# A graph-attention kernel: masks of two chunks made in place over a ring of six adjacency chunks, and a front with six row buffers

## What is computed

```
h    = relu(layernorm(x))
neib = tanh(neigh @ Wn1 + bn1) @ Wn2 + bn2            # 4096 x 32
val  = neigh @ Wv + bv                                # 4096 x 128
att  = tanh(h @ Wx1 + bx1) @ Wx2 + bx2                # 4096 x 32
ws   = leaky_relu(att @ neib.T, 0.01)                 # 4096 x 4096
ws   = softmax(where(adj > 0, ws, -9e15), axis=1)
out  = x + concat([h @ Wfx + bfx, ws @ val], axis=1)
```

## Time and profile before

| | |
|---|---|
| median of three runs | 505.74 us |
| the profiled execution: its own time, its span | 505.33 us, 503.5 us |
| TensorE matmul busy | 474.3 us (94%) |
| ScalarE busy | 434.8 us (86%) |
| VectorE busy | 425.3 us (84%) |
| GpSimd busy | 213.5 us (42%) |
| the masks, L663 | 128 instructions, 63.3 us and 1.7 us busy |

### The profile page before, as it was taken

The page is one execution under the profiler, slowest core; times in us unless marked ns, Lnnn a source line. Parts: engine busy times, 40 slices in busy tenths (PEclk is TensorE's granted clock), DMA queues, the critical chain, the costliest instruction groups (busy, mean ns, idle before and its releaser), DMA issues.

```text
span 503.5 us, 9162 instructions
## 1 busy us (share of the span) xinstructions
PE 474.3 (94%) x2964; PEld 368.3 (73%) x3007; DVE 425.3 (84%) x824; ACT 434.8 (86%) x625; POOL 213.5 (42%) x341
## 2 busy tenths in 40 slices
PE   6888898999999999999999999999999999998996
PEld 4767666776777677777777778777777787766884
DVE  1449898999898999999898989899998989994664
ACT  1675999999999899989999899989999999987552
POOL 1441042445644673457445663476445534540100
PEclk9999999999999999999999999999999999999999
DMA  8995475464567435755566356754564556500100
GB/s 232 269 217 105 102 127 87 78 141 77 85 120 172 77 59 100 159 111 86 78 133 142 67 85 126 168 83 62 97 142 81 85 105 125 85 1 1 43 2 21
DMA packets 38191, 52.04 MB, mean 103 GB/s; under 512 B 4096, under 2 KB 29952, under 8 KB 38144
## 3 DMA queue, kind: packets, MB, share of 16 engines
q0 software_dynamic: 9216, 33.56, 40.0%
q1 hardware_dynamic: 27856, 17.83, 11.8%
q10 hardware_dynamic: 1072, 0.07, 0.1%
HBM read 80.81 MB, written 4.19 MB: 169 GB/s over the span
## 4 chain that ended last, share of the span: by engine, by line
PE 64%; ACT 12%; issue 9%; DVE 8%; DMA 4%; POOL 2%; ACTq 1%; DVEq 0%; SPq 0%
PE ps_turned L924 17%; PE ps_scores L901 10%; PE ps_product L943 8%; PE ps_product L945 8%; PE ps_product L944 8%; PE ps_scores L900 4%; ACT pt_hi L516 3%; ACT scores L555 3%; ACT scores L543 3%; DVE scores L692 3%; PE ps_product L870 2%; DVE pt_lo L674 2%; DMA b<-in_L_gnn_bx 2%; POOL scores L419 2%; DMA x_left<-in_x 1%
## 5 line engine op out<-in xcount | busy, mean ns | idle before, releaser
L674 DVE TENSOR_TENSOR pt_lo<-ps_turned,pt_hi 128x512 fp32r<-128x512 f32 x256 | 172.9, 686 | 39.6 <-ACT pt_hi L516 20.6
L419 POOL TENSOR_TENSOR scores<-scores,mask 128x512 f32<-128x512 f32 x109 | 126.9, 1165 | 171.8 <-ACT scores L543 171.7
L516 ACT ACTIVATE pt_hi<-ps_turned 128x512 fp32r<-128x512 f32 x256 | 156.1, 610 | 37.7 <-PE ps_turned L924 37.2
L924 PE MATMUL ps_turned<-ident,scores 128*128 128x128 f32 x1024 | 154.6, 273 | 2.5 <-DVE pt_lo L674 2.3
L924 PEld LDWEIGHTS ps_turned<-ident,scores 128*128 128x128 f32 x1024 | 123.8, 140 | 44.2 <-DVE pt_lo L674 15.1
L543 ACT ACTIVATE scores<-ps_scores 128x1024 f32<-128x1024 f32 x128 | 132.4, 1035 | 5.7 <-PE ps_scores L901 5.7
L555 ACT ACTIVATE scores<-scores,neg_top 128x2048 f32<-128x2048 f32 x64 | 129.4, 2022 | 0.0
L692 DVE CUSTOM_DVE_ANT_0 scores<-ps_scores,scores,top 128x1024 f32<-128x1024 f32 x96 | 122.5, 1276 | 3.3 <-ACT scores L543 3.0
L943 PE MATMUL ps_product<-pt_hi,v_hi 128*128 128x512 f32 x256 | 122.1, 477 | 0.2 <-DVE pt_lo L674 0.2
L901 PE MATMUL ps_scores<-neib,xs 128*128 128x512 f32 x256 | 108.8, 502 | 3.7 <-DVE top L692 1.3
L945 PE MATMUL ps_product<-pt_lo,v_hi 128*128 128x512 f32 x256 | 101.4, 396 | 0.0
(11 more groups left out here) (76 smaller groups left out, 367.1 us busy)
## 6 DMA issues: line engine op xcount, KB each, us to landing
adj_in<-in_adj POOLq DMA_DIRECT2D x62, 512.0 KB, 5.4
scores<-in_L_gnn_neigh SPq DMA_DIRECT2D x8, 512.0 KB, 6.6
x_rows<-in_x SPq DMA_DIRECT2D x8, 512.0 KB, 3.7
x_left<-in_x SPq DMA_DIRECT2D x8, 256.0 KB, 6.7
x_right<-in_x SPq DMA_DIRECT2D x8, 256.0 KB, 2.9
out_h<-x_left SPq DMA_DIRECT2D x8, 256.0 KB, 3.4
out_h<-x_right SPq DMA_DIRECT2D x8, 256.0 KB, 3.4
scores<-in_adj POOLq DMA_DIRECT2D x2, 512.0 KB, 9.9
```

Source lines behind the costliest of these rows:

```text
L419: pool.tensor_tensor(half, half, mask[:, s % MASK_RING, BANK:CHUNK], ALU.add).then_inc(masked, 1)
L516: act.activation(pt_hi[:, (2 * b + u) % HI_RING], pt[:, u], ACT.Copy).then_inc(hi_done, 1)
L674: dve.tensor_tensor(pt_lo[:, u], pt[:, u], pt_hi[:, (2 * b + u) % HI_RING].bitcast(FP32), ALU.subtract).then_inc(lo_done, 1)
L924: last = pe.transpose(pt[:, u, i * P:(i + 1) * P], scores[:, parity * TILES + i, n * P:(n + 1) * P], ident[:, :])
```

## The change

The ring of masks goes. A mask of two chunks (2048 columns) is made by one VectorE instruction, in place over the two chunks of adjacency that one DMA has loaded, on even steps; TensorE and GpSimd read the masks there. The ring of adjacency has six chunks, and a pair is loaded anew when its scores and GpSimd's additions are done (on odd steps). The front has six row buffers; x_ahead is gone, and the statistics of x group 1 are made from x_rows, by VectorE in the last front step. The diagonal copies of the second-layer weights are made by VectorE from one small DMA each (spread_w2), most small weights move from ScalarE's queue to SyncE's, the wait for biases is split by side, ScalarE runs a Tanh on the identity before its first copy, and TensorE turns the identity some more times as filler (WARM_UP, FILL). The order of some pieces within a step changes on every engine, and the steps of the x work shift.

```diff
-ADJ_RING = 4
+ADJ_RING = 6
-MASK_RING = 3
-ROWS_RING = 5
+ROWS_RING = 6
-TURN_X = 5
-PACE = (4, 5, 6, 7)
+TURN_X = 4
+FILL = (6, 6, 4, 0, 0, 0, 0, 0)
-X_LOAD = -8
-X_STATS = (-6, -6, -6, -4)
+X_LOAD = -9
+X_STATS = (-6, -6, -5, -4)
-X_RSTD = (-3, -2, -1, -1)
-X_NORM = (0, 1, 2, 4)
+X_RSTD = (-4, -3, -2, -1)
+X_NORM = (2, 2, 4, 4)
-X_LEFT_LOAD, X_SUM = 11, (10, 13)
-X_RIGHT = 7
-V_START, V_STRIDE = 1, 2
+X_LEFT_LOAD, X_SUM = 16, (12, 14)
+X_RIGHT = 8
+V_START, V_STRIDE = 0, 2
+LEFT_0 = 4
-WARM_UP = 12
+WARM_UP = 15
...
+            def load_w2(side, w_in):
+                sp.dma_start(w2_raw[:, side, :], w_in.rearrange("(r p) h -> r p h", r=1).to_broadcast(
+                    [TILES, D_HID, D_HID])).then_inc(w2_in[side], 16)
...
# SyncE: n0 n1 x0 w2n n2 b2n n3 w1x n4 b1x w2x b2x n5, then n6, n7 as buffers come free, w_fx, w_v
+            sp.wait_ge(x_turned, KT)
+            load_x_rows(1)
# ... then the wide biases, x_left(0), x_right(0)
...
# GpSimd, front
+            pool.wait_ge(rows_in[(NEIGH_GROUPS - 2) % ROWS_RING], 32)
+            load_adj(0)
+            pool.wait_ge(rows_in[(NEIGH_GROUPS - 1) % ROWS_RING], 32)
+            load_adj(LOAD)
+            pool.wait_ge(x_rows_in, 32)
+            load_adj(2 * LOAD)
+            load_adj(3 * LOAD)
             for i in range(NEWTON + 1):
                 rstd_of(1, i)
+            load_adj(4 * LOAD)
...
# GpSimd, step: right_sum, left_sum, then the addition of the mask, then
+                gone = s - LOAD + 1
+                n = gone + ADJ_RING + (FRONT if gone < ADJ_RING else 0)
+                if gone % LOAD == 0 and 0 <= gone and n < STEPS and not ADJ_RING <= gone < ADJ_RING + FRONT:
+                    pool.wait_ge(scored, s + 1)
+                    if s >= POOL_MASKS:
+                        pool.wait_ge(masked, s + 1 - POOL_MASKS)
+                    load_adj(n)
...
# ScalarE, front: only w1_n and b1_n on its queue
+            act.wait_ge(made, 1)
+            act.activation(agg[:, 0:1], ident[:, 0:1], ACT.Tanh)
             turned_copy(0)
-            act.wait_ge(b1_in, B1_IN)
+            act.wait_ge(b1_in[0], 16)
...
# ScalarE, step: aggregate, hi 0, rise, hi 1, power, side
# VectorE, front step 7
+                if e == NEIGH_GROUPS - 1:
+                    for i in range(TILES):
+                        x_stats(1, i)
+                    x_aggr(1)
...
             def mask_of(n):
+                if n % LOAD or n >= STEPS:
+                    return
...
+                pair = adj_of(n, LOAD).rearrange("p a n -> p (a n)")
+                dve.tensor_scalar(pair, pair, 0.0, MASKED, ALU.is_le, ALU.mult).then_inc(mask_done, 1)
...
# VectorE, step: leak, lo 0, x_work, close, negate, lo 1, neigh_rest, mask_of(s + 2)
# TensorE: warm(FILL[e]) ahead of first_layer; product(s, -1) and agg_turn come ahead of side
-                    pe.wait_ge(mask_done, k + 1)
+                    pe.wait_ge(mask_done, s // LOAD + 1)
```

More of the change, by code:

```diff
@@ L107, in build @@
         adj_in = sb("adj_in", [P, ADJ_RING, CHUNK], BF16)
-        mask = sb("mask", [P, MASK_RING, CHUNK], BF16)
         xs = sb("xs", [P, 2, GROUP], FP32R)
@@ L148, in scratch @@
             return ap.rearrange(f"p ({names}) -> p {names}", **sizes)
-        rows = [scratch(4, i * TILES * D_IN, TILES, D_IN) for i in range(4)] + [scratch(5, 0, TILES, D_IN)]
-        x_ahead = scratch(5, 1024, TILES, D_IN)
+        rows = [scratch(4, i * TILES * D_IN, TILES, D_IN) for i in range(4)] + [scratch(5, i * TILES * D_IN, TILES, D_IN) for i in range(2)]
         hidden = scratch(5, 2048, 2, P)
@@ L242, in chunk_of, with adj_place, adj_of, mask @@
             return s // GSTEPS % 2, s // CHUNKS % TILES, s % CHUNKS
+        def adj_place(n):
+            return n if n < ADJ_RING else n - FRONT
+        def adj_of(n, chunks):
+            if ADJ_RING <= n < ADJ_RING + FRONT:
+                return adj_front[:, n - ADJ_RING:n - ADJ_RING + chunks, :]
+            i = adj_place(n) % ADJ_RING
+            return adj_in[:, i:i + chunks, :]
+        def mask(n):
+            return adj_of(n, 1).rearrange("p a n -> p (a n)")
         def v_halves(v, half):
@@ L413, in step @@
             def step(s):
+                for i in range(2):
+                    if (g := right_due(s - i)) is not None:
+                        right_sum(g, i)
+                for i in range(2):
+                    if e := x_due(s, X_SUM[i]):
+                        left_sum(e, i)
                 if POOL_MASKS <= s < STEPS:
@@ L418, in step @@
                     half = scores[:, parity * TILES + tile, c * CHUNK + BANK:(c + 1) * CHUNK]
-                    pool.tensor_tensor(half, half, mask[:, s % MASK_RING, BANK:CHUNK], ALU.add).then_inc(masked, 1)
-                n = s + ADJ_RING + (FRONT if s < FRONT else 0)
-                if s % LOAD == 0 and n < STEPS and not FRONT <= s < ADJ_RING + FRONT:
-                    pool.wait_ge(mask_done, s + LOAD)
-                    load_adj(n)
-                for i in range(2):
-                    if e := x_due(s, X_SUM[i]):
-                        left_sum(e, i)
-                for i in range(2):
-                    if (g := right_due(s - i)) is not None:
-                        right_sum(g, i)
+                    pool.tensor_tensor(half, half, mask(s)[:, BANK:CHUNK], ALU.add).then_inc(masked, 1)
+                gone = s - LOAD + 1
[4 more added lines that the diff above has]
+                        pool.wait_ge(masked, s + 1 - POOL_MASKS)
+                    load_adj(n)
                 for i in range(NEWTON + 1):
@@ L645, in _ @@
             x_aggr(0)
[L646 to L648 removed]
+            for side in range(2):
+                dve.wait_ge(b2_in[side], 16)
             def mask_of(n):
[L652 removed]
+                if n % LOAD or n >= STEPS:
+                    return
                 if ADJ_RING <= n < ADJ_RING + FRONT:
[L654 removed]
                     dve.wait_ge(front_ready[(n - ADJ_RING) // LOAD], 16)
                 else:
[L657 to L664 removed]
+                    dve.wait_ge(adj_ready[adj_place(n) % ADJ_RING // LOAD], 16 * (adj_place(n) // ADJ_RING + 1))
+                pair = adj_of(n, LOAD).rearrange("p a n -> p (a n)")
+                dve.tensor_scalar(pair, pair, 0.0, MASKED, ALU.is_le, ALU.mult).then_inc(mask_done, 1)
             def lo(s, u):
@@ L875, in _, with warm @@
             pe.wait_ge(made, 1)
-            for _ in range(WARM_UP):
-                pe.transpose(pa[:, 1, 0:P], ident[:, :], ident[:, :])
+            def warm(n):
+                for _ in range(n):
+                    pe.transpose(ps[:, 0, BANK:BANK + P], ident[:, :], ident[:, :])
+            warm(WARM_UP)
             turn_rows(0, 0)
@@ L899, in score @@
                 if not on_pool:
-                    pe.matmul(ps[:, s % 2, half], ident_bf16, mask[:, s % MASK_RING, half], start=True, stop=False)
+                    pe.matmul(ps[:, s % 2, half], ident_bf16, mask(s)[:, half], start=True, stop=False)
                 last = pe.matmul(ps[:, s % 2, half], xs[:, parity, tile * P:(tile + 1) * P],
@@ L982, in step @@
                 turn(s, 1)
-                side(s)
                 product(s, -1)
                 agg_turn(s)
+                side(s)
             for s in range(END):
```

118 lines of the change are left out of this document (54 added, 64 removed).

## The result

The changed kernel takes 507.3 us in the median of 20 runs, the kernel before 505.75 in 20 others beside it: ratio 1.0028, 95% interval 1.0016 to 1.0039. One of the 20, at 784.82 us with a granted clock of 0.56 throughout, is left out of the ratio. By the ratio that is 1.4 us slower, by the medians 1.55: at the edge of what was called no change, and clear of noise, where 498.0 was forecast. The profiled execution took 506.89 us, span 504.6, against 505.33 and 503.5.

What follows compares the result with a forecast made beforehand. Three near-equal engines, TensorE ahead, were taken to bound the loop, losing time where VectorE's masks and GpSimd collide. 505.33 - 4.2 (front) - 3.6 (loop) = 497.5, median 498.0; 8-in-10 range 492.5 to 502.5 us.

Steps and rivals of the forecast that it cites:

- Loop: The six full groups between 95 and 420 us: 0.6 us less each, 3.6 us in all.
- Net 1.46 - 0.85 = 0.6 us a group: Loop: TensorE's stalls of 1.46 us a group vanish, 0.85 us is newly exposed at even steps, 0.6 us is gained.
- Rival C: Loop: collisions leave, but 0.28 us appears at five more even steps; loop 0, front -4, 502 us; chance 0.12.
- rival D: Loop: pair ahead of even leaks fully exposed, still colliding with GpSimd; 2.2 us a group lost, 514 us; chance 0.06.
- Collisions: Loop: long VectorE masks beside GpSimd's tensor operations fall from three a group to one; excess of two is 1.32 us.
- Order within the step: Reordered pieces on TensorE, VectorE and ScalarE within a step: net 0, bounds -2 and +2 us.
- Adjacency loads: Loop: pairs reloaded at odd steps, about 8 us ahead of their mask, landing in 5.5 us median; hidden, cost 0.
- Front: Start of the kernel: last x step 4.9 us sooner, bounds 2 and 5.3; front in all -4.2 us.
- turn 3 starts at 13.3 to 14.9: Front: TensorE's turn of row group 3 starts 3.3 to 4.9 us sooner than its earlier 18.15 us.
- rival B: Front stays bound by DMA and its delayed statistics; front -1.5, loop -3, 501 us; chance 0.12.
- Given back: First steps after the last x step: statistics moved there make leak(4) 1.0 us later, ScalarE as bound there 0.7.

Runs made afterwards that it cites:

- all mends, single masks: The changed kernel with one mask instruction per chunk, group 0's four sums beside no mask, TensorE's idle time before turn 2 filled; 498.7 us, 0.9878.
- all mends, pair at odd steps: The changed kernel with mask pairs issued at odd steps, group 0's four sums beside no mask, TensorE's idle time before turn 2 filled; 498.95 us, 0.9885.

## Why the prediction was wrong

Sums of the gaps from leak to leak over 16 steps, mean of steps 32 to 111, in us:

```
                                  before even steps   before odd steps   period
kernel before                          30.5                23.6           54.1
after (pair ahead of even leaks)       32.7                21.4           54.1
after, but single masks                29.4                24.0           53.4
all mends, single masks                29.4                24.0           53.3
all mends, pair at odd steps           27.2                26.1           53.2
```

**Loop: -3.6 forecast, +0.4 measured (leak(18) to leak(114)).** The step that failed is "Net 1.46 - 0.85 = 0.6 us a group". Its cost side was nearly right: pairs ahead of even leaks cost 0.75 a group against single masks (0.85 assumed). In the table, the two kernels that differ in the pair alone have even gaps longer by 3.3 and odd ones shorter by 2.6, that is 0.4 and 0.3 a pair, where 0.28 later and 0.34 earlier were worked out; the difference is what the period loses. Its gain side was mis-sized. Everything else in the change is worth 0.85 a group (54.3 to 53.4), not 1.46. Of it the new orders are 0.15 or a little more; the ring gives nothing; the rest, the moved x work above all, has no run of its own. And a bound on it had been read: TensorE is busy 53.4 of 54.5 us in the earlier trace rows, so no edit beside it could take more than about 1.1 from the period. With the pair at odd steps TensorE is busy 54.40 of 54.50 and the period 53.28. Both come to 53.2 us of TensorE's work a group, by my estimate from these figures: the floor. The stalls in the earlier trace rows are idle time at the weight loads, and their 1.46 is more than the 1.1 for which the matmuls stood still, so they couldn't all come off the period. So 0.85 and 0.75 cancel. Rival C named this mechanism and its outcome ("0.28 us appears at five more even steps: loop 0"), at a chance of 0.12; rival D had the mechanism too, but at 2.2 us a group, where the pair costs 0.75 in this kernel and 1.1 on the kernel before.

**Collisions: "one collision a group where there are three".** Two pairs of 1.3 us a group stay. What the masks take over their price is 2.0 us a group before and 1.2 after, so there was a saving, and the period didn't follow it. The rule cited with rival D (the Trainium skill, "VectorE: DVE Perf Modes", section on two Vector instructions with no wait between them), that VectorE's second SBUF read interface is shared with GpSimd, and the traces agree: masks take 2.59 and 3.51 us beside sums back to back.

**Order within the step: 0 forecast, -1.9 measured.** Inside the bounds of 2, and part of the 0.85.

**Adjacency loads: 0 forecast, and no mask waits for one in the kernel after.** Right. The cover became thin only once the pair moved a step forward: VectorE waits 1.8 us for adjacency in the first of these kernels, 2.1 and 0.3 in the two others.

**Front: -4.9 at the last x step forecast, -1.7 measured.** What failed is "turn 3 starts at 13.3 to 14.9"; it started at 16.97. From there to the last x step it is 18.15 us (18.67 before), 0.5 less, as worked out (0.4). So the whole miss lies ahead of turn 3, in three parts. The sum took 4.9, near the upper end of its own 3.7 to 5.3 (3.3 to 4.9 up to turn 3, and 0.4 behind it), and so turn 2 at about 10.3; turn 2 came at 12.17, 1.9 later and just outside 10.3 to 11.9, since that row group is asked for at 3.04, behind the x rows and Wn2, where it was 2.31. From turn 2 to turn 3 it takes 3.25 at the full clock (3.0 assumed). And it took 1.5 more than that, since the fills don't bring the full clock to turn 2: the clock had been full (the first layer of group 0 took 0.64 us, that of group 1, behind the fall, 1.08) and was lost behind TensorE's wait of 2.92 us for those rows. The prediction had priced such a loss at 1.3 us and assumed it away. The clock isn't lost each time: in three profiled executions whose front up to there is the same (sums behind the addition, sums early, sums held), a wait of 2.56 to 2.87 us left the clock full and the last x step stands at 33.5 to 33.6. With the gap filled it stays full every time. The front's part of rival B, whose sign was turn 3 after 16 us, is what came.

**Given back: 0.7 forecast, 1.9 measured (last x step to leak(18): 48.3 before, 50.2 after).** The excess is one pair, 2.59 us where 0.69 was its price: with all mends and pairs, where it meets no sums, leak(18) comes 48.85 behind the last x step, so the pair costs 1.4 us there and the rest 0.5, near the 0.7. I had worked out where VectorE's statistics go and where GpSimd's rstd goes, but not that rstd, delayed by the statistics, pushes four sums onto a mask.

Together, as distances from the kernel before beside each: +1.55 us (after), 0.0 (sums early), -4.0 (pair at odd steps), -5.9 (sums placed beside no mask), -6.1 (gap filled), the last kernel with pairs. The 498.0 was within reach of these edits, but not of this change. The single steps carry what the clock did in each set of runs, so only the whole and the periods are firm. By its turns the filled gap is worth 1.5 us in an execution whose clock would fall and nothing in another, and placing the sums instead of only moving them early is worth 0.4 (leak(18) behind the last x step, 49.15 and 48.75, with pairs).

**Left open.** The last group is 0.75 us longer than before (53.55 against 52.79), with single masks still 0.3 (53.10); no run tells why. Nor does one tell why time less span is 2.25 us in the mean for every kernel with the ring of six, also on the front before, and 1.84 for the kernel before: 0.4 us that no span shows and the prediction didn't count. What makes the one load late wasn't tried.

## What to carry to other kernels

Before adding up stalls, cap what they can bring by the busy time of the fullest engine in that stretch: here 53.4 of 54.5 us left 1.1, whatever the stalls said. When two instructions become one, ask on which of the steps it lands: ahead of the steps that set the pace it cost 0.75 us a group, one step earlier it won 0.15. When one queue is delayed, follow everything behind it on that queue, down to what runs beside it on other engines; the four sums behind a late rstd took back most of what the front had won. And before crediting a gain to an edit, look whether TensorE's clock did the same in both executions: here one fall of it is 1.5 us, as much as most of the edits.

## What the runs showed of the hardware

- A mask on VectorE over two-byte SBUF columns is held for as long as GpSimd runs large tensor operations back to back: 0.42 us became 3.51, 0.69 became 2.59. The same sums leave statistics (1.40 for four) and PSUM-reading instructions (1.52 for two) as they are, and GpSimd's small rstd operations between 40 and 46 us left a pair at 0.69.
- TensorE's granted clock fell to the lower level in 13.4 to 16.8 us, behind an idle time of 2.92 us; with 20 idle transposes in it (1.19 us left) it stayed full, worth 1.5 us at the last x step. In other executions of the same front it stayed full behind 2.56 to 2.87 us of idle time. In the loop it fell behind 1.92 us, in a group with a late load, which took 56.52 us instead of 53.28; a like wait for the load without a fall cost 54.54.
- With pairs at odd steps, one load a group takes 1.00 us to issue instead of 0.58. One of them, at 247 us in both of the first such kernels, was awaited until 8.3 and 8.7 us behind its issue, where 5.5 is the median landing.
